# Layer 0 of a two-layer kernel rewritten: gate/up for tile pairs, values as the stationary operand, mask by identity rows, unrolled

## The reference

```python
xn = layernorm(x)
q, k, v = split(xn @ w_qkv.T)          # 32 query heads, 8 key/value heads, head size 64
q, k = rope(rmsnorm(q) * q_w, rmsnorm(k) * k_w)
probs = softmax(q @ k.T / 8 + mask)    # causal, sliding window of 64 keys
attn = (probs @ v) @ w_out.T
gate, up = xn @ Wg.T, xn @ Wu.T        # W = (int - 128) * scale, 704 hidden channels
ffn = (silu(gate) * up) @ Wd.T
x = x + attn + ffn
```

## Time and profile before

| | us |
|---|---|
| median of 3 runs | 1393.33 |
| lowest, highest | 1386.19, 1398.76 |
| the profiled execution: its own time | 1388.59 |
| its span, first to last instruction | 1386.8 |

### The profile page before, as it was taken

How to read it: one execution, slowest core, us unless ns; L and a number is a source line. 1 busy time by engine, 2 the same in 40 slices (tenths; PEclk the granted TensorE clock), 3 DMA queues, 4 the chain that set the end, 5 groups by cost and what they waited for, 6 DMA issues and landing times. The chain is left out here.

```text
span 1386.8 us, 30100 instructions
## 1 busy us (share of the span) xinstructions
PE 1172.2 (85%) x9946; PEld 775.5 (56%) x9946; DVE 893.8 (64%) x2105; ACT 690.9 (50%) x1632; POOL 677.4 (49%) x1067
## 2 busy tenths in 40 slices
PE   0399988888888898988988889718899999999998
PEld 0277877776776776766767768604333333333334
DVE  2776765665655656656656647366788888887841
ACT  1154434433433434434434334201699999987884
POOL 2386766766756757757757658330233333111000
PEclk9999999999998989999999989956899999999999
DMA  4300020110102201102201102240000000000000
GB/s 165 114 16 11 21 36 19 24 35 12 29 25 20 32 21 25 32 21 25 32 20 26 31 3 32 39 148 1 1 2 2 2 2 2 2 9 13 9 6 31
DMA packets 110229, 38.01 MB, mean 27 GB/s; under 512 B 93756, under 2 KB 108964, under 8 KB 109476
## 3 DMA queue, kind: packets, MB, share of 16 engines
q1 hardware_dynamic: 110076, 36.01, 12.1%
HBM read 19.25 MB, written 4.19 MB: 17 GB/s over the span
## 5 line engine op out<-in xcount | busy, mean ns | idle before, releaser
L1137 DVE TENSOR_REDUCE l_mxv<-l_mx 128x1 f32<-128x1024 f32 x256 | 306.4, 1221 | 63.8 <-PE l_mx L1323 60.6
L1025 ACT ACTIVATE l_prob<-l_sc 128x512 f32<-128x512 f32 x512 | 285.9, 597 | 48.8 <-PE l_sc L1330 46.2
L634 POOL TENSOR_TENSOR t<-t 128x320 f32<-128x320 f32 x128 | 110.3, 861 | 244.4 <-DVE t L518 240.7
L1323 PE MATMUL l_mx<-l_kt,l_qt 48*128 48x512 f16 x512 | 179.2, 396 | 8.6 <-DVE l_mxv L1137 6.9
L517 DVE TENSOR_TENSOR t<-qk,tcw 128x320 f32<-128x320 f32 x128 | 62.5, 489 | 187.0 <-ACT v L375 186.9
L1330 PE MATMUL l_sc<-l_qt,l_kt 50*128 50x512 f16 x512 | 177.2, 386 | 0.0
L783 PE MATMUL ob<-wo,ats 128*128 128x256 f32 x512 | 143.2, 405 | 36.9 <-DVE xc L587 36.9
L1190 POOL TENSOR_SCALAR l_mxs<-l_mxv 128x8 f32<-128x8 f32 x32 | 7.5, 233 | 319.9 <-DVE l_mxv L1137 319.9
L1303 PE MATMUL l_acc<-l_prob,qkv_all 128*17 128x256 f32 x2048 | 161.4, 388 | 0.1
L626 POOL TENSOR_TENSOR rm<-ve,half_neg 128x5 f32<-128x5 f32 x128 | 150.1, 1173 | 0.1
L764 PE MATMUL pv<-v,probs 128*128 128x65 f32 x1024 | 129.3, 270 | 0.0
(11 more groups left out here) (177 smaller groups left out, 2680.4 us busy)
## 6 DMA issues: line engine op xcount, KB each, us to landing
qkv_all<-qs SPq DMA_DIRECT2D x16, 256.0 KB, 3.8
v<-v SPq DMA_DIRECT2D x240, 16.2 KB, 1.7
qkv_all<-w_qkv SPq DMA_DIRECT2D x1, 3072.0 KB, 10.2
xn_all<-xs SPq DMA_DIRECT2D x16, 128.5 KB, 2.0
wo<-w_o SPq DMA_DIRECT2D x1, 2048.0 KB, 15.0
xa<-x SPq DMA_DIRECT2D x16, 128.0 KB, 2.3
xc<-x SPq DMA_DIRECT2D x16, 128.0 KB, 2.6
out<-xc SPq DMA_DIRECT2D x16, 128.0 KB, 2.2
```

The costliest lines, as they stand in the source:

```text
L634: pool.tensor_tensor(t1[:, b, :, :], t1[:, b, :, :], t2[:, :, :], ALU.add).then_inc(s_["pool_u"], 1)
L1025: act.activation(prob[:, (y * NI + u) % NPR, h * 512:(h + 1) * 512], sc[:, k % NSC, :], ACT.Exp, scale=D1 ** -0.5).then_inc(s_["act_sc"], 1)
L1137: dve.tensor_reduce(mxv[:, x % 2, u:u + 1], mx[:, MX[k] % 2, :], AX.X, ALU.max).then_inc(s_["dve_mx"], 1)
L1323: ins = pe.matmul(mx[:, MX[kx] % 2, keys], qt[r:r + KS, x // 2 % 4, u * P:(u + 1) * P], kt[r:r + KS, x // 2 % 4, keys], start=True, stop=True)
```

## The change

- The hidden channels of gate and up are taken in 6 chunks of 128 (the last of 64) in place of 8 groups of 88. Each chunk is done for a pair of tiles at once (the tiles at the same place of the two sequences), so the moving operand has 256 columns. A chunk comes every second slot, 6 in the 16 slots of a pair. The down product has 6 steps a tile, in the groups 2 to 7.
- The values are the stationary operand (64 columns) and the probabilities move (128 columns). The output comes out transposed, two heads one above the other in the partitions. A second product with a 64-column block of ones gives the sums, once for every output element. DVE takes the reciprocal of all 256 columns and multiplies; PE's transposes and ACT's evacuation of them are gone.
- The second score product uses 64 rows of the keys and queries (no duplicated low part). The mask is added by a product over the other 64 rows, whose partner is rows of the identity. The halves lie in two banks; the 64-row products stand in pairs, one on the lower and one on the upper rows, the first pair before the value products and the second behind them. The mask tile isn't rewritten any more.
- The norm's transposes and the layer-1 projection have a bank of their own (`extra`); the projection has one bank (`qk`) in place of two.
- DVE copies the high part of the keys (128 x 64 in place of 128 x 128) before POOL's low parts are done, and doesn't wait for them. The rope tables are built once a pair.
- All slots are written out, and most lags are one slot (4, 5, 6, 7, 8, 9), so a slot's step needs what other engines did in the slot before.

The core of the diff:

```diff
-LAG_A = 8
-LAG_N = 9
-LAG_T = 10
-LAG_S = 11
-LAG_V = 13
-LAG_O = 14
-LAG_W = 15
+LAG_A = 4
+LAG_F0 = 4
+LAG_N = 5
+LAG_T = 6
+LAG_S = 7
+LAG_V = 8
+LAG_W = 9
+WD_K = 2
...
+            for s in TIMES:
...
+                    wait(pe, s_["act_A"], n * G + k)
+                    wait(pe, s_["dve_A"], n * G + k)
                     for c in range(KC):
                         for j, (a, w) in enumerate(((xh, wq_hi), (xh, wq_lo), (xl, wq_hi))):
-                            ins = pe.matmul(BANK(k)[:, 0:CW], a[:, t.par, c, :], w[:, c, k, :],
+                            ins = pe.matmul(qk[:, 0:CW], a[:, i % 2, c, b, :], w[:, c, k, :],
                                             start=(c == 0 and j == 0), stop=(c == KC - 1 and j == 2))
...
-                                ins = pe.matmul(ffv[0:HP, u, :], w[:, c, k, u, :], a[:, t.par, c, :],
+                                ins = pe.matmul(ff[0:m, u, :, :], w[:, c, u, cols], a[:, i % 2, c, :, :],
                                                 start=(c == 0 and j == 0), stop=(c == KC - 1 and j == 2))
...
+                    pe.matmul(weights[0], keys(n, k, 1, 0, top), queries(k, 0, top), start=True, stop=False)
+                    pe.matmul(weights[1], outside(n, 1), eyes, start=True, stop=False)
+                    pe.matmul(weights[0], keys(n, k, 0, 0, full), queries(k, 0, full), start=False, stop=False)
+                    pe.matmul(weights[1], keys(n, k, 0, 1, full), queries(k, 1, full), start=False, stop=False
+                              ).then_inc(s_["pe_S1"], 1)
...
                     for h, v in enumerate((v0, v1)):
                         for a in range(2):
-                            ins = pe.matmul(pvv[:, 2 * h + a, :], pm[:, b, h, 2 * a:2 * a + 2, :], v[:, t.par, k, :],
+                            pe.matmul(pvo[a * HD:(a + 1) * HD, :, h, :], v[:, bb, k, :], pm[:, b, h, 2 * a:2 * a + 2, :],
+                                      start=True, stop=True)
+                    for h in range(2):
+                        for a in range(2):
+                            ins = pe.matmul(pvs[a * HD:(a + 1) * HD, :, h, :], one[:, :], pm[:, b, h, 2 * a:2 * a + 2, :],
                                             start=True, stop=True)
                     ins.then_inc(s_["pe_V"], 1)
...
+                    pe.wait_ge(s_["pe_S1"], n * G + k + 1)
+                    pe.matmul(weights[0], outside(n, 0), eyes, start=False, stop=True)
+                    pe.matmul(weights[1], keys(n, k, 1, 1, top), queries(k, 1, top), start=False, stop=True
+                              ).then_inc(s_["pe_S"], 1)
...
+                    dve.wait_ge(s_["act_hi"], n * G + k + 1)
+                    wait(dve, s_["pe_T"], n * G + k - 1)
+                    dve.tensor_copy(nat[:, b, REP, HD:P], nat[:, b, REP, 0:HD]).then_inc(s_["dve_dup"], 1)
...
+                    dve.wait_ge(s_["pe_V"], n * G + k + 1)
+                    wait(dve, s_["dve_an"], n * G + k)
+                    dve.reciprocal(rc[:, :, :], pv[:, 256:512].rearrange("p (j t) -> p j t", j=2)).then_inc(s_["dve_rc"], 1)
+                    dve.wait_ge(s_["dve_rc"], n * G + k + 1)
+                    wait(dve, s_["pe_W"], n * G + k - 1)
+                    dve.tensor_tensor(ats[:, b, :, :], pv[:, 0:256].rearrange("p (j t) -> p j t", j=2), rc[:, :, :], ALU.mult
+                                      ).then_inc(s_["dve_an"], 1)
```

More of the change, by code:

```diff
@@ L133, in build, with chunk, at, pair_tile @@
         layer1(nc, idf, xn2_all, qkv1_all, w_out1, b_r, w1, b1, w2, b2, before, fold, slots, out)
+def chunk(f):
+    return slice(f * P, min(HID, (f + 1) * P)), min(HID - f * P, P)
+def at(slot, lag):
+    n, k = divmod(slot - lag, G)
+    return n, k, 0 <= n < NT
+def pair_tile(slot):
+    t, g = divmod(slot, G)
+    return t + g // 2 if g in (0, 2) and t % 2 == 0 and 0 <= t < NT else None
+def wait(eng, sem, count):
+    if count > 0:
+        eng.wait_ge(sem, count)
 def layer0(nc, whole, idf, xn2_all, qkv1_all, x, w_qkv, w_o, q_w, k_w, w_gate, w_up, s_gate, s_up, w_down, s_down,
@@ L449, in _ @@
[L449 removed]
+                if ok:
+                    act.wait_ge(s_["pe_S"], n * G + k + 1)
+                    wait(act, s_["pe_V"], n * G + k - 1)
+                    act.activation(pm[:, b, :, :, :], sc[:, :, 0:REP * WIN].rearrange("p h (r q) -> p h r q", r=REP), ACT.Exp,
+                                   bias=neg_bound[:, 0:1], scale=HD ** -0.5).then_inc(s_["act_exp"], 1)
         @block.vector
@@ new lines, in _, with keys, queries, outside @@
+            eyes = idh[low, HD:P].unsqueeze(1).broadcast_to([HD, REP, WIN])
+            weights = [sc[:, h, 0:REP * WIN].rearrange("p (r q) -> p r q", r=REP) for h in range(2)]
+            def keys(n, k, j, h, rows):
+                return kts[rows, n % B, j, k, h * WIN:h * WIN + P]
+            def queries(k, h, rows):
+                return qt[rows, k % 2, :, h * WIN:(h + 1) * WIN]
+            def outside(n, h):
+                return mk[low, 0 if n < B and h == 0 else 1, :]
+            for s in TIMES:
+                g = s % G
+                n, k, ok = at(s, LAG_A)
+                if ok:
+                    i, b = n // B, n % B
+                    pe.wait_ge(s_["dve_xl"], n + 1)
+                    wait(pe, s_["act_A"], n * G + k)
+                    wait(pe, s_["dve_A"], n * G + k)
@@ L725, in slot @@
+                i = (s - LAG_F0) // 16
+                if s >= LAG_F0 and s % 2 == LAG_F0 % 2 and f < NF and i < NI:
+                    cols, m = chunk(f)
+                    pe.wait_ge(s_["dve_xl"], i * B + 2)
+                    wait(pe, s_["dve_h"], i * NF + f)
                     for u in range(2):
@@ new lines, in _ @@
+                n, k, ok = at(s, LAG_W)
+                b = k % 2
+                if ok:
+                    pe.wait_ge(s_["dve_an"], n * G + k + 1)
+                    if k == 0:
+                        wait(pe, s_["dve_x1"], n)
+                    for j in range(2):
+                        ins = pe.matmul(ob[:, 0:D], ats[:, b, j, :], wo[:, k, j, :], start=(k == 0 and j == 0),
+                                        stop=False)
+                    f = k - WD_K
+                    if f >= 0:
+                        m = chunk(f)[1]
+                        pe.wait_ge(s_["dve_h"], n // B * NF + f + 1)
+                        ins = pe.matmul(ob[:, 0:D], ht[0:m, f, n % B, :], wd[0:m, f, :], start=False, stop=(k == G - 1))
+                    ins.then_inc(s_["pe_W"], 1)
```

714 lines of the change are left out of this document (307 added, 407 removed).

## The result

The changed kernel takes 1422.41 us (median of 4 runs, 1414.65 to 1424.83). The kernel before, run beside it, takes 1396.05 (1386.19 to 1402.68). The ratio is 1.0185, with a 95% interval of 1.011 to 1.0261: the change makes the kernel slower by nearly 2%. I had put 1397, slower by over 1% with a chance of 0.37, and no change or faster with 0.63. The time lies inside the range of 1345 to 1445, but outside the likeliest case's own range (1370 to 1418), and a slowdown clear of zero stands where I had put next to none.

What follows compares the result with a forecast made beforehand. The bound was to move from PE to DVE, at 51.4 us a tile plus 0.8 idle. 57.6 + 816 + 8 + 13 + 23 = 918 us to layer 1, 8 later than now, gave 1397 us; range 1345 to 1445.

Steps and rivals of the forecast that it cites:

- likeliest case: Whole kernel: DVE-bound at 50.5 to 53.5 us a tile, 1370 to 1418 us, chance 0.50.
- I take 2.32: DVE's reciprocal of 256 elements a row: 2.32 us, from 173 ns for 4 elements plus 252 at 8.5 ns.
- DVE's sum: DVE's work a tile: 44.2 for eight slots, 2.6 for chunks, 4.6 for norms and the rest, 51.4 us.
- The bound moves from PE to DVE: After the change DVE, at 51.4 us a tile, sets the pace instead of PE, at 42.1.
- I put 0.8 us a tile for such places and those I don't see: DVE's idle time where layer-1 projection meets a chunk, and in unseen places: 0.8 us a tile, making 52.2.
- The check of DVE's slot: Next rope product can start 4.4 us after the scaling; DVE comes at 5.53, so 1.1 us to spare.
- SP's two value transfers a slot have three slots until they are used: SP's queue: the two value transfers issued each slot have three slots until their use.
- The clock: its rival: PE waits up to 1 us a slot halve the granted clock a third of the time: as much as 1450 us.
- The key's copy: DVE's key copy ahead of POOL's low parts: 0.10 us of work plus 0.35 average wait behind POOL, each slot.
- the copy doesn't wait: Rival: DVE's key copy isn't held by POOL, 45 us less, 1352 us; copy free or DVE otherwise below 50.5: chance 0.17.
- PE's floor: PE's work a tile after the change: 42.1 us, bounds 37.7 with free division changes and 49.0 without column-half overlap.
- The single banks: Single `qk` and `pv` banks cost nothing, with 1.1 us to spare in a slot.

Runs made afterwards that it cites:

- e7_b_big: The kernel before the change, with a reciprocal of 256 elements a row in place of 4 and the same result: 1493.1 us, ratio 1.0699.
- e3_both: The changed kernel with a separate buffer for the unread router-weight product and the value carry issued three slots earlier: 1316.27 us, ratio 0.943 to the kernel before.
- e6_both_small: e3_both with a reciprocal of 4 elements a row in place of 256, normalisation left out: 1261.92 us, ratio 0.9043 to the kernel before.
- e10_act_copy: e3_both with the copy of the rotated key on ACT instead of DVE: 1314.67 us, ratio 0.942 to the kernel before.
- e1_prod: The changed kernel with the unread router-weight product (L547) written to its own buffer: 1343.92 us, ratio 0.9639 to the kernel before.
- e2_carry: The changed kernel with the transfer of the carried values issued three slots earlier on SP's queue: 1388.41 us, ratio 0.9956 to the kernel before.

## Why the prediction was right and where it was wrong

The time fell into the range because two errors of opposite sign nearly cancelled. That is luck: what turned a gain into a loss, the two stops, stands in none of its steps.

**The size of the reciprocal: the term was mis-sized.** The step "I take 2.32", from the 34 ns between the earlier trace rows, is 1.746 measured (e7_b_big: 1.749). 0.575 us by 8 are 4.6 us a tile too much. The two rows were of 4 and of 8 elements and of different tiles, and their slope of 8.5 was carried 248 elements further. At 32 to 128 elements the slope is 6.25. The fixed part of 94 ns found there would give a 4-element one 119 ns and an 8-element one 144, but they take 173 and 197: the short ones don't lie on that line, and two short ones don't give its slope. The Trainium skill (VectorE: DVE Perf Modes, Walkthrough: the 8-slice pipeline in each mode) has the divide repeat 8 times; the estimate from it was 8.3 ns an element and 2.27 us in all. The trace disagrees, with 6.25 ns and 1.746 us, and the measurement decides.

**DVE's sum: right but for that term.** 51.4 less 4.6 are 46.8, and 47.6 with the 0.8 of idle time. e3_both, in which the two missed waits are away, takes 47.5 us a tile with DVE at 93%. By distances of starts that is 45.4 of work and 2.1 of waiting for ACT, so two small errors (1.4 too much, 1.3 too little) also cancel in the match. "The bound moves from PE to DVE" holds for the reciprocal in that kernel (e6_both_small), but not for every step on DVE's list (e10_act_copy); in the changed one no engine is the bound.

**DVE's idle time: the step that failed.** "I put 0.8 us a tile for such places and those I don't see" misses 8.4 us: 55.9 in the changed kernel less the 47.5 of e3_both. The check of DVE's slot compared it with PE's banks only, for the steps that every slot has. The norm steps were counted as durations (4.6 a tile) and their waits weren't held against PE's list. L547's wait for `pe_xat` stands in the code, one line above the instruction, and the two lists give its price: the instruction that releases it is in slot g = 4 at the end of PE's list, the one that waits in slot g = 3 at the end of DVE's. One slot. e1_prod prices it at 78 us.

**SP: the step that failed.** "SP's two value transfers a slot have three slots until they are used" is true of PE, which reads them at the value product. It isn't true of ACT, which may overwrite `v1` only behind the carry, in the same slot. The edit was costed for its reader and not for the next writer of its source. e2_carry prices it at 34 us. Nor was SP's list walked with its waits: the changed L275 stands behind stores that wait for POOL.

**The two errors cancelled.** In a tile of the steady stretch they are -4.6 and +8.4 us: 56 where 52.2 was forecast. Over the whole layer they are -74 (0.575 x 128) and +109: the last residual sum comes at 918.31 us, and at 809.18 in e3_both. That is less than 16 x 8.4, since the tiles at both ends have no stop or a smaller one. The two leave +35, and the profiled execution is 28 above its forecast (1424.8 against 1396.6); the other -7 are small errors in the start, the fill, the drain and the tail. The range held the time, but the mechanism that made the kernel slower was among none of the rivals.

**The clock: its rival was argued away wrongly.** That "the half clock follows waits of 2 us and more" fits the kernel before but for one fall: between 200 and 750 us twelve stand at stops of PE of 2.3 to 2.7 us, and one, at 392 us, behind stops of 1.54 and 1.50. In the changed kernel the clock falls to 0.50 behind stops of 1.42 and 1.24 us, and at 550 us of e3_both even behind 0.62 and 1.09. Its mean between 200 and 750 us is 0.95 before, 0.92 in the changed kernel and 0.99 in e3_both, so what the change lost of it came with the two stops. What it costs alone no run separates.

**The key's copy: the size right, the place wrong.** The step had 0.45 us a slot. Starts 0.58 us apart without a chunk (503.75 to 504.33 in e3_both) and 0.14 behind one (407.25 to 407.39 in the changed kernel) make 0.42 over ten and six slots of sixteen. The copy ends where POOL's rounding ends, at 271.2 us in the changed kernel:

```profile
270.49 0.69 POOL L585 TENSOR_TENSOR nat<-t,nat 128x256 f16<-128x256 f32 x1
270.57 0.65 DVE L499 COPY nat<-nat 128x64 f16<-128x64 f16 x1
```

So POOL did hold the copy, as the epsilon step of the earlier trace rows suggested. By the Trainium skill (SBUF — State Buffer, Who interferes with whom), a DVE copy can take a port pair that it shares with POOL, and whoever comes second waits until the first instruction is over; the trace agrees, with 464 ns behind POOL's rounding and 242 at the end of the slot. But the step put those 0.45 us on the path, and e10_act_copy shows, on top of e3_both, that they aren't there: the 0.69 us between the carried keys and the queries are set by ACT's eviction. The sum stayed right, since the wait for ACT, which it didn't have, is as long as the copy, which it had. In e3_both the rival "the copy doesn't wait" would thus have gained nothing; in the changed kernel itself it wasn't tried.

**PE: right within 2 us a tile.** The column halves run two at a time, and each change of the array's division takes about 0.1 us. PE's timeline of the changed kernel:

```profile
400.60 0.28 PE L701 MATMUL sc<-qt,kts 64*128 64x256 f16 x1
400.60 0.28 PE L702 MATMUL sc<-idh,mk 64*128 64x256 f16 x1
400.81 0.28 PE L703 MATMUL sc<-qt,kts 128*128 128x256 f16 x1
400.93 0.27 PE L704 MATMUL sc<-qt,kts 128*128 128x256 f16 x1
401.13 0.66 PE L716 MATMUL pv<-probs,v 128*64 128x128 f32 x8
401.62 0.61 PE L720 MATMUL pv<-probs,one 128*64 128x128 f32 x8
402.16 0.28 PE L726 MATMUL sc<-idh,mk 64*128 64x256 f16 x1
```

A pair of half products to a whole one is 0.21 us, of which 0.108 is the product. The sixteen value records take 1.03 us from 401.13 to 402.16, with one change in it, where 0.87 + 0.11 = 0.98 was the step and 1.73 its upper bound. PE's floor was put at 42.1 us a tile; e6_both_small, with PE 98 to 99% busy, runs at 43.9. Which term is short isn't known.

**The single banks: right for the common slot.** `qk` and `pv` "cost nothing" as long as nobody is late. After a late DVE they hand the delay on: the 1.42 us at 405.57 are PE's wait for the single `qk` bank.

## What to carry to other kernels

When work is moved between slots, hold every wait in the code against the place of its releaser on the other engine's list, the waits of once-a-tile steps too, and for a DMA also the next writer of its source; a buffer that only takes a result nobody reads should be shared with nothing. A long instruction is on the path only if no chain as long runs beside it: look for who else would have been waited for, before you count it or take it away. And don't carry a slope far beyond the two rows that give it.

## What was not expected of the hardware

RECIPROCAL of fp32 from PSUM costs 6.25 ns an element at 32 to 128 elements (294, 494, 894 ns) and 1746 ns at 256, while 4 and 8 elements take 173 and 197. Cutting one into five costs 0.05 us in all, since starts overlap. The issue of a load on SP's queue, 0.59 us in the median, took 2.09 right behind two stores of 0.63 and 1.04, and the small carry takes 2.08 in that place (328.30). So it is the place and not the transfer that makes it long; why, the runs don't show. And the granted clock fell to 0.50 behind two stops that were each under 1.5 us.
